# Cross-attention block: the last 82 context rows multiplied in two contraction tiles instead of three products

## The chip, the cores and the metric

The kernel runs on one core of one Trainium2 chip. The metric is the device time of that core in microseconds (us). The kernel before takes 300.28 us (median of 3 runs, 299.73 to 300.45); one further run was recorded by the hardware profiler, and all rows in this document come from that one.

## What is computed

For each of B = 8 batches there are N = 100 query rows of width D = 1024 and M = 722 context rows of width C = 512. Cut to what matters:

```python
memory_proj = einsum('bme,de->bmd', memory, W_mem)
scores = einsum('bnd,bmd->bnm', hidden_states, memory_proj) / sqrt(D)
attn = softmax(scores, axis=-1)
memory_context = einsum('bnm,bmd->bnd', attn, memory_proj)
gate = sigmoid(einsum('bnf,df->bnd', concat([hidden_states, memory_context]), W_gate) + b_gate)
out = rmsnorm(hidden_states + gate * memory_context, norm_w)
```

The kernel never forms `memory_proj`. It multiplies the queries with `W_mem` first (giving `q`, width 512), takes scores against the raw context, multiplies the probabilities with the raw context (giving 100 x 512 per batch, called `pc`), and multiplies that with `W_mem` afterwards (giving `mc`). The step that is changed is probabilities times raw context: for each batch a product over 722 context rows.

## The kernel before

**Three products for one.** Every large float32 product is made from operands split in two: `hi` is the operand copied by ScalarE (ACT) into the narrower format float32r, `lo` is what remains (operand minus `hi`, by VectorE, DVE), also float32r. A product is `hi*hi + hi*lo + lo*hi`, three matmuls on TensorE (PE) that accumulate in one PSUM bank.

**Stages.** First the query projection (to 42.4 us), then `for b in range(B): step(b, ...)`, one batch each, then the projection to `mc`, the gate and the normalisation. In a step PE runs, in this order: scores (L384, 24 matmuls), some matmuls of the gate's x half to fill time (`fill(1)`, L290), the six transposes of the probabilities (L398), `fill(2)` (L290), the probabilities times the context (L408), `fill(3)` (L290), four transposes of `pc` (L415). The fills run over 3, 3 and 1 of 8 blocks; in step 0 they run over 3, 2 and 1, with 2 ahead of the scores.

**The product over 722 rows.** 722 rows are `MT = 5` tiles of 128 and a last one of `ML = 82`. Each tile costs three matmuls, 18 in all; each streams 512 columns, whether the tile has 128 rows or 82. PE waits for `pt_lo_done` ahead of tile 0 and for `cn_lo_done` ahead of tiles 0 and 3.

**Who makes the operands.** The context rows are loaded into `cn_stage` by DMAs that SyncE (SP) issues: tiles 0 to 2 (L217), tiles 3 and 4 (L221), the 82 rows (L223). ACT makes `cn_hi` (L542 for tiles 0 to 2; L545 and L546 for the rest) and DVE `cn_lo` (all its subtractions have the helper's line, L711). The probabilities come transposed out of PSUM: ACT writes `pt_hi` (L600 for five tiles, L602 for the 82 rows, `pt_hi_done`), then DVE `pt_lo` (`pt_lo_done`). In step b ACT's order is: exponential, a weight split (L523), L545, L546, L600, L602, the two `ct_hi` (L534, the transposed context for the next step's scores), then `pc` (L607). DVE's order is: maxima, weight split, `pt_lo`, `cn_lo` of tiles 3 to 5, the two `ct_lo`.

**SP's order.** SP issues one DMA after another, and waits in place. For batch b + 1: a gate weight, two halves of `ct_stage` (L210), L217, then (after `cn_lo_done` of batch b's second part, since the buffer is single) L221 and L223. After the last batch's context come the weights `w_mem_t` 1 to 3.

Of the kernel before, what the change touches and what calls it, by code (L numbers as in the profile page):

```python
# [5 lines left out]
B, N, D = 8, 100, 1024  # L6
M, C = 722, 512
# [3 lines left out]
KD, KC = D // P, C // P  # L11
MT = M // P
ML = M - MT * P
MH = M // 2
BANK = 512
WB = KD * P
# [26 lines left out]
def build(nc, xT, ctxT, ctxN, w_mem, w_gate_x, w_mem_t, w_gate_mc, b_gate, norm_w, outT, out_rows):  # L43
# [4 lines left out]
    with top:  # L48
# [18 lines left out]
        bias_t = sb(top, "bias_t", [P, KD])  # L67
        norm_t = sb(top, "norm_t", [P, KD])
        table_probe = sb(top, "table_probe", [P, 1])
        idle_work = sb(top, "idle_work", [P, P], mybir.dt.bfloat16)  # L70
        top_score = sb(top, "top_score", [N, 2])
        neg_top = sb(top, "neg_top", [N, 1])
# [3 lines left out]

        with ExitStack() as attn:
            ct_stage = sb(attn, "ct_stage", [P, KC, M])
            cn_stage = sb(attn, "cn_stage", [P, MT + 1, C])
            ct_hi = sb(attn, "ct_hi", [P, KC, M], F32R)  # L80
            ct_lo = sb(attn, "ct_lo", [P, KC, M], F32R)
            cn_hi = sb(attn, "cn_hi", [P, MT + 1, C], F32R)
            cn_lo = sb(attn, "cn_lo", [P, MT + 1, C], F32R)
            probs = sb(attn, "probs", [N, M])
            pt_hi = sb(attn, "pt_hi", [P, MT + 1, N], F32R)
            pt_lo = sb(attn, "pt_lo", [P, MT + 1, N], F32R)
            pc = sb(attn, "pc", [N, C])
# [56 lines left out]
        first_hi_done, first_lo_done = sem("first_hi_done"), sem("first_lo_done")  # L144
        ct_hi_done, ct_lo_done = sem("ct_hi_done"), sem("ct_lo_done")
        cn_hi_done, cn_lo_done = sem("cn_hi_done"), sem("cn_lo_done")
        q_hi_done, q_lo_done = sem("q_hi_done"), sem("q_lo_done")
        pt_hi_done, pt_lo_done = sem("pt_hi_done"), sem("pt_lo_done")
        at_hi_done, at_lo_done = sem("at_hi_done"), sem("at_lo_done")
# [45 lines left out]
        @block.sync  # L195
        def _(sp):
            def load_x(k):
                sp.dma_start(acc[:, k, :], xT[k * P:(k + 1) * P, :]).then_inc(x_in[k], 16)

            def load_w(j, src, slot):  # L200

                if not isinstance(j, int) or j >= 2:
                    sp.wait_ge(w_lo_done, j - 1)
                sp.dma_start(w_stage[:, slot, :], src).then_inc(w_in[slot], 16)

            def load_ctxT(b, first=False):
                for s in range(2):
                    if not first:
                        sp.wait_ge(ct_lo_done, 2 * b - 1 + s)
                    sp.dma_start(ct_stage[:, 2 * s:2 * s + 2, :],  # L210
                                 ct_rows[bass.ds(b * C + s * 2 * P, 2 * P), :]
                                 .rearrange("(k p) m -> p k m", p=P)).then_inc(ct_in[s], 16)

            def load_ctx(b, first=False):
                if not first:
                    sp.wait_ge(cn_lo_done, 2 * b - 1)
                sp.dma_start(cn_stage[:, 0:3, :], cn_rows[bass.ds(b * M, 3 * P), :]  # L217
                             .rearrange("(t p) c -> p t c", p=P)).then_inc(cn_in[0], 16)
                if not first:
                    sp.wait_ge(cn_lo_done, 2 * b)  # L220
                sp.dma_start(cn_stage[:, 3:MT, :], cn_rows[bass.ds(b * M + 3 * P, (MT - 3) * P), :]  # L221
                             .rearrange("(t p) c -> p t c", p=P)).then_inc(cn_in[1], 16)
                sp.dma_start(cn_stage[0:ML, MT, :],  # L223
                             cn_rows[bass.ds(b * M + MT * P, ML), :]).then_inc(cn_in[1], 16)


            sp.dma_start(acc[:, 0, 0:H], xT[0:P, 0:H]).then_inc(x_first_in, 16)
            for i in range(2):
                cols = slice(i * C // 2, (i + 1) * C // 2)
                sp.dma_start(w_stage[:, 0, cols], w_mem[0][:, cols]).then_inc(w_first_in[i], 16)  # L230
            sp.dma_start(acc[:, 0, H:R], xT[0:P, H:R]).then_inc(x_in[0], 16)
            sp.dma_start(w_stage[:, 0, C:WB], w_mem[0][:, C:WB]).then_inc(w_in[0], 16)
            sp.dma_start(acc[:, 1, 0:H], xT[P:2 * P, 0:H]).then_inc(x_second_in, 16)
            sp.dma_start(acc[:, 1, H:R], xT[P:2 * P, H:R]).then_inc(x_in[1], 16)
            load_x(2)
            load_w(1, w_mem[1], 1)
            load_x(3)
            load_x(4)
            load_x(5)
            load_w(2, w_mem[2], 0)  # L240
            load_x(6)
            load_x(7)
            load_w(3, w_mem[3], 1)
            load_ctxT(0, first=True)
            load_ctx(0, first=True)
            sp.dma_start(bias_t[:, :], b_gate).then_inc(const_in, 16)
            sp.dma_start(norm_t[:, :], norm_w).then_inc(const_in, 16)
            load_w(J_GX, w_gate_x[0], 0)
            load_w(J_GX + 1, w_gate_x[1], 1)


            def ahead(b, slot):
                load_w(J_GX + 2 + b, wgx_rows[bass.ds((b + 2) * P, P), :], slot)
                load_ctxT(b + 1)
# [12 lines left out]

            sp.wait_ge(mc_made, 1)
            sp.dma_start(x_again[:, :, :], xT.rearrange("(k p) r -> p k r", p=P)).then_inc(xa_in, 16)
            for t in range(1, KD):  # L270
                load_w(J_G2 + t, w_gate_mc[t], t % 2)
            for k in range(0, KD, 2):
                sp.wait_ge(out_done, k + 2)
                sp.dma_start(out_v[:, k:k + 2, :], acc[:, k:k + 2, 0:FIRST]).then_inc(stored, 16)
            for i in range(ROWS2):
                sp.wait_ge(row_left, i + 1)
                sp.wait_ge(row_right, i + 1)
                sp.dma_start(out_rows[i * CHUNK:(i + 1) * CHUNK, :],
                             row_out[:, i * D:(i + 1) * D]).then_inc(stored, 16)
            sp.wait_ge(stored, 16 * (KD // 2 + ROWS2))  # L280
# [3 lines left out]
        def _(pe):  # L284
# [80 lines left out]
            def step(b, slot, cuts):  # L365
# [34 lines left out]
                fill(2)  # L400

                pe.wait_ge(pt_lo_done, b + 1)
                for t in range(MT + 1):
                    if t in (0, 3):
                        pe.wait_ge(cn_lo_done, 2 * b + 1 + t // 3)
                    rows = P if t < MT else ML
                    for lhs, rhs, part in ((pt_hi, cn_hi, 0), (pt_hi, cn_lo, 1), (pt_lo, cn_hi, 2)):
                        done = nc.tensor.matmul(bank(PCB, C, N), lhs[0:rows, t, :], rhs[0:rows, t, :],  # L408
                                                start=t == 0 and part == 0, stop=t == MT and part == 2)
                done.then_inc(pc_made, 1)  # L410
                fill(3)

# [102 lines left out]
        def _(act):  # L515
# [21 lines left out]
            def split_ctx(b, part):  # L537
                if part == 0:
                    if not isinstance(b, int) or b > 0:
                        act.wait_ge(pc_made, b)  # L540
                    act.wait_ge(cn_in[0], 16 * b + 16)
                    nc.scalar.activation(cn_hi[:, 0:3, :], cn_stage[:, 0:3, :], ACT.Copy).then_inc(cn_hi_done, 1)  # L542
                else:
                    act.wait_ge(cn_in[1], 32 * b + 32)
                    nc.scalar.activation(cn_hi[:, 3:MT, :], cn_stage[:, 3:MT, :], ACT.Copy)  # L545
                    nc.scalar.activation(cn_hi[0:ML, MT, :], cn_stage[0:ML, MT, :],  # L546
                                         ACT.Copy).then_inc(cn_hi_done, 1)

            act.wait_ge(x_first_in, 16)
            nc.scalar.activation(act_hi[:, 0, 0:H], acc[:, 0, 0:H], ACT.Copy).then_inc(first_hi_done, 1)  # L550
# [158 lines left out]
        def _(dve):  # L709
# [18 lines left out]
            def split_ctx(b, part):  # L728
                dve.wait_ge(cn_hi_done, 2 * b + part + 1)
                if part == 0:  # L730
                    minus(cn_lo[:, 0:3, :], cn_stage[:, 0:3, :], cn_hi[:, 0:3, :]).then_inc(cn_lo_done, 1)
                else:
                    minus(cn_lo[:, 3:MT, :], cn_stage[:, 3:MT, :], cn_hi[:, 3:MT, :])
                    minus(cn_lo[0:ML, MT, :], cn_stage[0:ML, MT, :], cn_hi[0:ML, MT, :]).then_inc(cn_lo_done, 1)

            nc.vector.memset(idle_work[:, :], 0.0).then_inc(idle_work_set, 1)
            dve.wait_ge(first_hi_done, 1)
# [19 lines left out]
            split_x(6)  # L757
            split_x(7)
            split_w(3, 1)
            split_ctxT(0)  # L760
            split_ctx(0, 0)
            split_ctx(0, 1)
# [157 lines left out]
        def _(pool):  # L920
            nc.gpsimd.memset(ident[:, :], 0.0).then_inc(ident_zeroed, 1)
            pool.wait_ge(ident_zeroed, 1)
            nc.gpsimd.affine_select(out=ident[:, :], in_=ident[:, :], compare_op=ALU.not_equal, fill=1.0,
                                    base=0, pattern=[[-1, P]], channel_multiplier=1).then_inc(consts_set, 1)


            pool.wait_ge(mean_w_set, 4)
# [36 lines left out]
```

## Time and profile before

| what | value |
|---|---|
| median of 3 runs | 300.28 us (299.73 to 300.45) |
| the profiled run, its time | 300.07 us |
| its span (first to last instruction) | 298.3 us |
| PE busy | 292.5 us (98%), 1674 matmuls |
| ACT busy | 156.4 us (52%) |
| DVE busy | 164.1 us (55%) |
| TensorE clock granted, mean | 0.996 of full |
| chain that ended last | PE 98%, of which L290 69%, L408 11%, L384 11% |

The profile's chain of waits goes back from the last instruction to whatever released each one. Matmuls overlap in the pipeline, so one is recorded as about 0.39 us long while the next starts 0.23 us after it. The cost of one matmul in a stream is the distance between starts, or the length of a piece of the chain by its count, never the recorded duration. "PEld" is the loading of a matmul's stationary operand, which runs beside the matmul before it. "SPq" rows are DMA issues on SP.

### The profile page before, as it was taken

The page shows a single profiled execution, that of the slowest core. Times are in us where ns is not written, and L with a number is a line of the kernel's source. Part 1 is how long each engine was busy: PE and PEld are TensorE (multiplying, and loading weights), DVE is VectorE, ACT ScalarE, POOL GpSimd, SP SyncE. Part 2 cuts the span into 40 slices and gives each one's busy share as a digit, 9 for nine tenths or more (in the row PEclk, how much of TensorE's full clock was granted, in tenths as well). Part 3 has the DMA queues.
Part 4 walks back from the last instruction along what each step waited for, and adds up shares of the span by engine and source line. Part 5 has one row for each costly group of instructions (what it writes and reads, how often), then busy time and mean ns, then how long its engine had stood idle before and what let it go on. Part 6 is the DMA issues. An engine that isn't in the chain of part 4 may idle for free.

```text
span 298.3 us, 4078 instructions
## 1 busy us (share of the span) xinstructions
PE 292.5 (98%) x1674; PEld 281.3 (94%) x1674; DVE 164.1 (55%) x232; ACT 156.4 (52%) x227; POOL 3.0 (1%) x9
## 2 busy tenths in 40 slices
PE   8999999999999999999999999999999999999993
PEld 8999999898999989899898989999999999999993
DVE  3657454557575565855557553423457662543663
ACT  5547345454573736548363525543467773643563
POOL 0000000000000000000000000000000000010001
PEclk9999999999999999999999999999999999999998
DMA  6998391644729467383944020177223400000235
GB/s 207 406 369 268 105 357 34 229 132 135 243 99 313 149 210 247 98 265 116 288 182 145 20 70 8 64 286 294 74 70 142 141 2 1 0 2 8 109 114 211
DMA packets 18450, 46.34 MB, mean 155 GB/s; under 512 B 1520, under 2 KB 3312, under 8 KB 18432
## 3 DMA queue, kind: packets, MB, share of 16 engines
q1 hardware_dynamic: 18432, 46.09, 45.2%
q8 instruction: 13, 0.21, 0.3%
q14 instruction: 5, 0.04, 0.0%
HBM read 42.80 MB, written 3.28 MB: 154 GB/s over the span
## 4 chain that ended last, share of the span: by engine, by line
PE 98%; DVE 0%; issue 0%; DVEq 0%
PE ps L290 69%; PE ps L408 11%; PE ps L384 11%; PE ps L398 1%; PE ps L304 1%; PE ps L415 1%; PE ps L488 1%; PE ps L315 0%; PE ps L318 0%; PE ps L476 0%; DVE x_again L911 0%; PE ps L325 0%; PE ps L330 0%; PE ps L321 0%; PE ps L327 0%; PE ps L468 0%
## 5 line engine op out<-in xcount | busy, mean ns | idle before, releaser
L290 PE MATMUL ps<-act_hi,w_hi 128*128 128x400 f32 (+4 forms) x272 | 79.5, 342 | 0.0
L290 PE MATMUL ps<-act_hi,w_lo 128*128 128x400 f32 (+4 forms) x272 | 78.9, 340 | 0.0
L290 PE MATMUL ps<-act_lo,w_hi 128*128 128x400 f32 (+4 forms) x272 | 78.8, 340 | 0.0
L290 PEld LDWEIGHTS ps<-act_hi,w_hi 128*128 128x128 f32 x272 | 49.9, 188 | 0.9
L290 PEld LDWEIGHTS ps<-act_lo,w_hi 128*128 128x128 f32 x272 | 50.6, 188 | 0.1
L290 PEld LDWEIGHTS ps<-act_hi,w_lo 128*128 128x128 f32 x272 | 50.6, 188 | 0.0
L711 DVE TENSOR_TENSOR w_lo<-w_stage,w_hi 128x1024 fp32r<-128x1024 f32 (+2 forms) x23 | 26.0, 1131 | 24.3 <-ACT w_hi L523 23.2
L711 DVE TENSOR_TENSOR cn_lo<-cn_stage,cn_hi 128x1536 fp32r<-128x1536 f32 (+2 forms) x24 | 28.6, 1217 | 6.4 <-ACT cn_hi L542 5.6
L711 DVE TENSOR_TENSOR ct_lo<-ct_stage,ct_hi 128x1444 fp32r<-128x1444 f32 x16 | 25.8, 1654 | 0.5 <-ACT ct_hi L534 0.5
L523 ACT ACTIVATE w_hi<-w_stage 128x1024 fp32r<-128x1024 f32 x20 | 21.0, 1054 | 6.7 <-PE ps L290 4.9
L607 ACT ACTIVATE pc<-ps,row_inv 100x512 f32<-100x512 f32 x8 | 5.5, 687 | 34.3 <-PE ps L408 34.3
L534 ACT ACTIVATE ct_hi<-ct_stage 128x1444 fp32r<-128x1444 f32 x16 | 21.7, 1408 | 0.0
L664 ACT ACTIVATE gate<-ps,bias_t 128x384 f32<-128x384 f32 (+3 forms) x15 | 8.6, 570 | 24.6 <-PE ps L290 24.5
L384 PE MATMUL ps<-ct_hi,q_hi 128*100 128x362 f32 x64 | 21.4, 334 | 0.0
L593 ACT ACTIVATE probs<-ps,neg_top 100x722 f32<-100x722 f32 x8 | 6.9, 865 | 27.2 <-DVE neg_top L782 27.2
L384 PE MATMUL ps<-ct_hi,q_lo 128*100 128x362 f32 x64 | 21.0, 328 | 0.0
L849 DVE TENSOR_TENSOR gate<-gate,mc 128x416 f32<-128x416 f32 (+3 forms) x17 | 9.3, 550 | 21.1 <-ACT gate L664 21.1
L384 PE MATMUL ps<-ct_lo,q_hi 128*100 128x362 f32 x64 | 20.9, 327 | 0.0
L711 DVE TENSOR_TENSOR act_lo<-mc,act_hi 128x800 fp32r<-128x800 f32 x8 | 7.9, 993 | 20.5 <-ACT mc L635 20.5
L408 PE MATMUL ps<-cn_hi,pt_hi 128*100 128x512 f32 (+1 forms) x48 | 18.9, 394 | 0.0
L408 PE MATMUL ps<-cn_hi,pt_lo 128*100 128x512 f32 (+1 forms) x48 | 18.8, 392 | 0.0
L408 PE MATMUL ps<-cn_lo,pt_hi 128*100 128x512 f32 (+1 forms) x48 | 18.8, 391 | 0.0
(105 smaller groups left out, 446.2 us busy)
## 6 DMA issues: line engine op xcount, KB each, us to landing
ct_stage<-ctxT SPq DMA_DIRECT2D x16, 722.0 KB, 9.8
cn_stage<-ctxN SPq DMA_DIRECT2D x8, 768.0 KB, 5.8
cn_stage<-ctxN SPq DMA_DIRECT2D x8, 512.0 KB
w_stage<-w_gate_x SPq DMA_DIRECT2D x8, 512.0 KB, 8.9
w_stage<-w_gate_mc SPq DMA_DIRECT2D x8, 512.0 KB, 3.6
x_again<-xT SPq DMA_DIRECT2D x1, 3200.0 KB, 11.3
acc<-xT SPq DMA_DIRECT2D x6, 400.0 KB, 7.9
w_stage<-w_mem_t SPq DMA_DIRECT2D x4, 512.0 KB, 5.6
```

Source lines behind the costliest of these rows:

```text
L290: done = nc.tensor.matmul(o, wgt, stream[h][part], start=first and wgt is wh and part == 0, stop=last and wgt is wl, skip_group_check=onto)
L304: nc.tensor.matmul(bank(7, P), idle_work[:, :], idle_work[:, :], start=True, stop=True)
L384: done = nc.tensor.matmul(bank(h, MH + 1, N), lhs[:, k, b * N:(b + 1) * N], rhs[:, k, at:at + MH + 1], start=k == 0 and part == 0, stop=k ...
L398: done = nc.tensor.transpose(o, probs[:, t * P:t * P + rows], ident[0:N, 0:N])
L408: done = nc.tensor.matmul(bank(PCB, C, N), lhs[0:rows, t, :], rhs[0:rows, t, :], start=t == 0 and part == 0, stop=t == MT and part == 2)
L523: nc.scalar.activation(w_hi[home][:, :], w_stage[:, slot, :], ACT.Copy).then_inc(w_hi_done, 1)
L534: nc.scalar.activation(ct_hi[:, 2 * s:2 * s + 2, :], ct_stage[:, 2 * s:2 * s + 2, :], ACT.Copy).then_inc(ct_hi_done, 1)
L593: nc.scalar.activation(probs[:, :].rearrange("p (h m) -> p h m", h=2), scores, ACT.Exp, bias=neg_top[:, :], scale=float(D) ** -0.5, accum_ ...
L607: nc.scalar.activation(pc[:, :], bank(PCB, C, N), ACT.Copy, scale=row_inv[:, :]).then_inc(pc_scaled, 1)
L664: nc.scalar.activation(part, part if n < 2 else gate_bank(n), ACT.Sigmoid, bias=bias_t[:, t:t + 1]).then_inc(gate_done, 1)
L711: return nc.vector.tensor_tensor(out, whole, hi.bitcast(F32), ALU.subtract)
L849: nc.vector.tensor_tensor(part, part, mc[:, t, r0:r1], ALU.mult).then_inc(gated, 1)
```

## The change

The three products of the last 82 rows have 3 x 82 = 246 rows to contract, and these fit into two tiles of up to 128 rows. With `SPILL = 42` and `REST = 40`:

- tile `MT`: rows 0 to 81 are `pt_hi` against `cn_hi`; rows 82 to 123 are `pt_hi` of rows 0 to 41 against `cn_lo` of rows 0 to 41
- tile `MT + 1`: rows 0 to 81 are `pt_lo` against `cn_hi`; rows 82 to 121 are `pt_hi` of rows 42 to 81 against `cn_lo` of rows 42 to 81

The context side is loaded from memory in this layout (82 rows twice, by a broadcast source, and once more as 42 and 40 rows at partition 82): four DMAs in place of one. ACT writes `sign * stage` over 124 rows x 1024 columns, with sign -1 in rows below 82 and +1 above; DVE then writes `stage * low_rows - that` in place, which is `hi` below row 82 and `lo` above. The probabilities' side is made as before, and two small DMAs inside SBUF copy `pt_hi` rows to partition 82 onward of `pt_hi` and `pt_lo` (`move_pt`); PE waits for both (`pt_moved`) ahead of the last two matmuls. `low_rows` and `hi_sign` are computed once on DVE, and GpSimd zeroes the spare rows once.

```diff
@@ sync
+            def move_pt(b):
+                sp.wait_ge(pt_hi_done, b + 1)
+                sp.dma_start(pt_hi[ML:ML + SPILL, MT, :].bitcast(F32),
+                             pt_hi[0:SPILL, MT, :].bitcast(F32)).then_inc(pt_moved, 16)
+                sp.dma_start(pt_lo[ML:ML + REST, MT, :].bitcast(F32),
+                             pt_hi[SPILL:ML, MT, :].bitcast(F32)).then_inc(pt_moved, 16)
...
                 if not first:
+                    move_pt(b - 1)
                     sp.wait_ge(cn_lo_done, 2 * b)
                 sp.dma_start(cn_stage[:, 3:MT, :], cn_rows[bass.ds(b * M + 3 * P, (MT - 3) * P), :]
                              .rearrange("(t p) c -> p t c", p=P)).then_inc(cn_in[1], 16)
-                sp.dma_start(cn_stage[0:ML, MT, :],
-                             cn_rows[bass.ds(b * M + MT * P, ML), :]).then_inc(cn_in[1], 16)
+                at = b * M + MT * P
+                if first:
+                    sp.wait_ge(spare_zeroed, 1)
+                for a, n in ((0, ML - 2), (ML - 2, 2)):
+                    sp.dma_start(cn_stage[a:a + n, MT:MT + 2, :], cn_rows[at + a:at + a + n, :].unsqueeze(1)
+                                 .to_broadcast([n, 2, C])).then_inc(cn_end_in, 16)
+                sp.dma_start(cn_stage[ML:ML + SPILL, MT, :], cn_rows[at:at + SPILL, :]).then_inc(cn_end_in, 16)
+                sp.dma_start(cn_stage[ML:ML + REST, MT + 1, :],
+                             cn_rows[at + SPILL:at + ML, :]).then_inc(cn_end_in, 16)
...
             load_w(J_MC + 1, w_mem_t[1], 1)
+            move_pt(B - 1)
             load_w(J_MC + 2, w_mem_t[2], 0)
@@ tensor
-                for t in range(MT + 1):
+                for t in range(MT):
                     if t in (0, 3):
                         pe.wait_ge(cn_lo_done, 2 * b + 1 + t // 3)
...
+                pe.wait_ge(pt_moved, 32 * (b + 1))
+                for i, (lhs, rows) in enumerate(((pt_hi, ML + SPILL), (pt_lo, ML + REST))):
+                    done = nc.tensor.matmul(bank(PCB, C, N), lhs[0:rows, MT, :], cn_hi[0:rows, MT + i, :],
+                                            start=False, stop=i == 1)
@@ scalar
-                    act.wait_ge(cn_in[1], 32 * b + 32)
+                    act.wait_ge(cn_in[1], 16 * b + 16)
                     nc.scalar.activation(cn_hi[:, 3:MT, :], cn_stage[:, 3:MT, :], ACT.Copy)
-                    nc.scalar.activation(cn_hi[0:ML, MT, :], cn_stage[0:ML, MT, :],
-                                         ACT.Copy).then_inc(cn_hi_done, 1)
+                    act.wait_ge(cn_end_in, 64 * b + 64)
+                    act.wait_ge(hi_sign_set, 1)
+                    rows = slice(0, ML + SPILL)
+                    nc.scalar.activation(cn_hi[rows, MT:MT + 2, :], cn_stage[rows, MT:MT + 2, :], ACT.Copy,
+                                         scale=hi_sign[rows, :]).then_inc(cn_hi_done, 1)
@@ vector
-                    minus(cn_lo[0:ML, MT, :], cn_stage[0:ML, MT, :], cn_hi[0:ML, MT, :]).then_inc(cn_lo_done, 1)
+                    packed = cn_hi[0:ML + SPILL, MT:MT + 2, :]
+                    nc.vector.scalar_tensor_tensor(packed, cn_stage[0:ML + SPILL, MT:MT + 2, :],
+                                                   low_rows[0:ML + SPILL, :], packed.bitcast(F32), ALU.mult,
+                                                   ALU.subtract).then_inc(cn_lo_done, 1)
...
+            dve.wait_ge(consts_set, 1)
+            nc.vector.reduce_sum(low_rows[:, :], ident[:, ML:P], AX.X).then_inc(low_rows_set, 1)
+            dve.wait_ge(low_rows_set, 1)
+            nc.vector.tensor_scalar(hi_sign[:, :], low_rows[:, :], 2.0, -1.0, ALU.mult, ALU.add)\
+                .then_inc(hi_sign_set, 1)
@@ gpsimd
+            pool.wait_ge(consts_set, 1)
+            nc.gpsimd.memset(cn_stage[96:P, MT:MT + 2, :], 0.0).then_inc(spare_zeroed, 1)
```

On PE, the end of the product over the context in step 0, before (the last three are the 82-row tile, L290 is `fill(3)`, L415 the transposes of `pc`):

```order
L408 MATMUL ps<-cn_hi,pt_lo 100x512
L408 MATMUL ps<-cn_hi,pt_hi 100x512
L408 MATMUL ps<-cn_lo,pt_hi 100x512
L408 MATMUL ps<-cn_hi,pt_lo 100x512
L290 MATMUL ps<-act_hi,w_hi 128x400 x2
L290 MATMUL ps<-act_lo,w_hi 128x400 x2
L290 MATMUL ps<-act_hi,w_lo 128x400 x2
L415 MATMUL ps<-ident,pc 128x100 [waits pc_scaled]
```

The same place after (L431 is the old L408, L435 the packed tiles, L314 the old L290, L442 the old L415):

```order
L431 MATMUL ps<-cn_hi,pt_lo 100x512
L435 MATMUL ps<-cn_hi,pt_hi 100x512 [waits pt_moved]
L435 MATMUL ps<-cn_hi,pt_lo 100x512
L314 MATMUL ps<-act_hi,w_hi 128x400 x2
L314 MATMUL ps<-act_lo,w_hi 128x400 x2
L314 MATMUL ps<-act_hi,w_lo 128x400 x2
L442 MATMUL ps<-ident,pc 128x100 [waits pc_scaled]
```

One matmul of three is gone, and the first of the two that remain waits for the moved rows.

On SP, the issues of one steady step, before:

```order
L204 DMA w_stage<-w_gate_x 128x1024 [waits w_lo_done]
L210 DMA ct_stage<-ctxT 128x2x722 [waits ct_lo_done] x2
L217 DMA cn_stage<-ctxN 128x3x512 [waits cn_lo_done]
L221 DMA cn_stage<-ctxN 128x2x512 [waits cn_lo_done]
L223 DMA cn_stage<-ctxN 82x512
```

and after:

```order
L211 DMA w_stage<-w_gate_x 128x1024 [waits w_lo_done]
L217 DMA ct_stage<-ctxT 128x2x722 [waits ct_lo_done] x2
L232 DMA cn_stage<-ctxN 128x3x512 [waits cn_lo_done]
L224 DMA pt_hi<-pt_hi 42x100 [waits pt_hi_done]
L226 DMA pt_lo<-pt_hi 40x100
L237 DMA cn_stage<-ctxN 128x2x512 [waits cn_lo_done]
L243 DMA cn_stage<-ctxN 80x2x512
L243 DMA cn_stage<-ctxN 2x2x512
L245 DMA cn_stage<-ctxN 42x512
L246 DMA cn_stage<-ctxN 40x512
```

Two small copies stand between the two context loads, and four loads stand where one stood.

## Rows read from the trace of the kernel before

**Rows 1.** The page, part 1 (busy us, share, instructions) and part 2.
```profile
PE 292.5 (98%) x1674; PEld 281.3 (94%) x1674; DVE 164.1 (55%) x232; ACT 156.4 (52%) x227; POOL 3.0 (1%) x9
...
PEclk9999999999999999999999999999999999999998
```

**Rows 2.** The chain that ended last: start us, us, what (step 3, then step 4).
```profile
105.55 4.13 PE ps L408 x18
109.68 1.09 PE ps L290 x6
...
123.25 4.18 PE ps L408 x18
```

**Rows 3.** The instructions of L408, one of three alike: duration ns, forms.
```profile
L408 PE MATMUL ps<-cn_hi,pt_hi x48: 389/394/398, 52.3 to 179.7; 128*100 128x512 f32 x40, 82*100 82x512 f32 x8
```

**Rows 4.** Timeline of step 3, loads of PE's stationary operand: start us, us.
```profile
105.21 0.16 PEld L408 LDWEIGHTS ps<-cn_hi,pt_hi 128*100 128x100 f32 x1
...
107.23 0.16 PEld L408 LDWEIGHTS ps<-cn_hi,pt_hi 128*100 128x100 f32 x1
...
108.60 0.16 PEld L408 LDWEIGHTS ps<-cn_hi,pt_hi 82*100 82x100 f32 x1
...
110.87 0.17 PEld L384 LDWEIGHTS ps<-ct_hi,q_hi 128*100 128x100 f32 x1
```

**Rows 5.** Timeline of step 3, ACT and DVE: start us, us, idle before.
```profile
101.44 0.62 ACT L546 ACTIVATE cn_hi<-cn_stage 82x512 fp32r<-82x512 f32 x1
102.30 0.59 ACT L600 ACTIVATE pt_hi<-ps 128x500 fp32r<-128x500 f32 x1 [0.23 <-PE ps L398]
102.78 0.24 ACT L602 ACTIVATE pt_hi<-ps 82x100 fp32r<-82x100 f32 x1
...
103.06 0.84 DVE L711 TENSOR_TENSOR pt_lo<-ps,pt_hi 128x500 fp32r<-128x500 f32 x2 [1.13 <-ACT pt_hi L602]
103.82 1.81 DVE L711 TENSOR_TENSOR cn_lo<-cn_stage,cn_hi 128x1024 fp32r<-128x1024 f32 x2
105.56 3.22 DVE L711 TENSOR_TENSOR ct_lo<-ct_stage,ct_hi 128x1444 fp32r<-128x1444 f32 x2
```

**Rows 6.** Groups by shape: busy us, mean ns, idle before.
```profile
L711 DVE TENSOR_TENSOR cn_lo<-cn_stage,cn_hi 128x1024 fp32r<-128x1024 f32 x8 | 9.7, 1213 | 0.8 <-ACT cn_hi L546 0.8
...
L711 DVE TENSOR_TENSOR cn_lo<-cn_stage,cn_hi 82x512 fp32r<-82x512 f32 x8 | 5.4, 680 | 0.0
...
L545 ACT ACTIVATE cn_hi<-cn_stage 128x1024 fp32r<-128x1024 f32 x8 | 8.4, 1053 | 1.4 <-DMA cn_stage<-ctxN 1.4
...
L546 ACT ACTIVATE cn_hi<-cn_stage 82x512 fp32r<-82x512 f32 x8 | 4.9, 616 | 0.0
```

**Rows 7.** Timeline of step 3, the issues on SP around `cn_lo`.
```profile
97.55 0.37 SPq L217 DMA_DIRECT2D cn_stage<-ctxN  x1
105.66 0.37 SPq L221 DMA_DIRECT2D cn_stage<-ctxN  x1
```

**Rows 8.** Timeline of step 0: the end of `pt_hi`, the first 82-row load.
```profile
50.80 0.24 ACT L602 ACTIVATE pt_hi<-ps 82x100 fp32r<-82x100 f32 x1
...
55.53 0.16 PEld L408 LDWEIGHTS ps<-cn_hi,pt_hi 82*100 82x100 f32 x1
```

**Rows 9.** DMA issues: count, KB each, median us from issue to landing.
```profile
ct_stage<-ctxT SPq DMA_DIRECT2D x16, 722.0 KB, 9.8
cn_stage<-ctxN SPq DMA_DIRECT2D x8, 768.0 KB, 5.8
...
outT<-acc SPq DMA_DIRECT2D x4, 416.0 KB, 2.5
```

**Rows 10.** Windows: busy by engine (PE, PEld, DVE, ACT, POOL), clock, DMA share, GB/s.
```profile
104.00:105.00 1.00, 1.00 (x7) 1.00 (x6) 1.00 (x2) 1.00 (x2) 0.00 (x0) 1.00 0.00 0
115.00:116.00 1.00, 1.00 (x7) 1.00 (x6) 1.00 (x3) 0.00 (x0) 0.00 (x0) 1.00 0.14 53
```

**Rows 11.** Timeline of DVE ahead of step 0: idle time before the first `q_lo`.
```profile
37.07 1.13 DVE L711 TENSOR_TENSOR q_lo<-ps,q_hi 128x400 fp32r<-128x400 f32 x2 [3.06 <-ACT q_hi L584]
```

More of the change, by code:

```diff
@@ L13 @@
 ML = M - MT * P
+SPILL, REST = 42, ML - 42
 MH = M // 2
@@ L69, in build @@
         table_probe = sb(top, "table_probe", [P, 1])
+        low_rows = sb(top, "low_rows", [P, 1])
+        hi_sign = sb(top, "hi_sign", [P, 1])
         idle_work = sb(top, "idle_work", [P, P], mybir.dt.bfloat16)
@@ L78, in build @@
             ct_stage = sb(attn, "ct_stage", [P, KC, M])
-            cn_stage = sb(attn, "cn_stage", [P, MT + 1, C])
+            cn_stage = sb(attn, "cn_stage", [P, MT + 2, C])
             ct_hi = sb(attn, "ct_hi", [P, KC, M], F32R)
             ct_lo = sb(attn, "ct_lo", [P, KC, M], F32R)
-            cn_hi = sb(attn, "cn_hi", [P, MT + 1, C], F32R)
-            cn_lo = sb(attn, "cn_lo", [P, MT + 1, C], F32R)
+            cn_hi = sb(attn, "cn_hi", [P, MT + 2, C], F32R)
+            cn_lo = sb(attn, "cn_lo", [P, MT, C], F32R)
             probs = sb(attn, "probs", [N, M])
@@ L146, in build @@
         cn_hi_done, cn_lo_done = sem("cn_hi_done"), sem("cn_lo_done")
+        spare_zeroed, low_rows_set, hi_sign_set = sem("spare_zeroed"), sem("low_rows_set"), sem("hi_sign_set")
+        cn_end_in, pt_moved = sem("cn_end_in"), sem("pt_moved")
         q_hi_done, q_lo_done = sem("q_hi_done"), sem("q_lo_done")
@@ L402, in step @@
                 pe.wait_ge(pt_lo_done, b + 1)
-                for t in range(MT + 1):
+                for t in range(MT):
                     if t in (0, 3):
                         pe.wait_ge(cn_lo_done, 2 * b + 1 + t // 3)
-                    rows = P if t < MT else ML
                     for lhs, rhs, part in ((pt_hi, cn_hi, 0), (pt_hi, cn_lo, 1), (pt_lo, cn_hi, 2)):
-                        done = nc.tensor.matmul(bank(PCB, C, N), lhs[0:rows, t, :], rhs[0:rows, t, :],
-                                                start=t == 0 and part == 0, stop=t == MT and part == 2)
+                        nc.tensor.matmul(bank(PCB, C, N), lhs[:, t, :], rhs[:, t, :],
+                                         start=t == 0 and part == 0, stop=False)
+                pe.wait_ge(pt_moved, 32 * (b + 1))
+                for i, (lhs, rows) in enumerate(((pt_hi, ML + SPILL), (pt_lo, ML + REST))):
+                    done = nc.tensor.matmul(bank(PCB, C, N), lhs[0:rows, MT, :], cn_hi[0:rows, MT + i, :],
+                                            start=False, stop=i == 1)
                 done.then_inc(pc_made, 1)
```

## The prediction

> **What bounds the kernel now.** I read the page first, then the chain of waits, then one steady step (step 3, 93.4 to 111.1 us) in the timeline. The page shows PE busy 98% of the span while ACT and DVE are busy about half, and the clock row shows full speed in nearly every slice [rows 1]. So TensorE runs at its upper level of 2.4 GHz with nothing to win or lose there. The chain of waits is PE work from end to end, and its pieces follow each other without a gap: in step 3 the product over the context starts at 105.55 and takes 4.13 us, and `fill(3)` starts at 109.68, which is 105.55 + 4.13 [rows 2]. PE is the bound in each of the 8 steps. A matmul taken out of this stream is therefore worth its full spacing, as long as nothing that PE waits for comes later than PE wants it. The rest of the argument is how much room each such operand has.
>
> **What is removed.** L408 has 3 x 48 matmuls, 8 of each 48 with 82 rows, and these take as long as those with 128 (one range of 389 to 398 ns for both forms) [rows 3]. The spacing is 4.13 us / 18 = 0.2294 us (0.2322 in step 4) [rows 2]. One of 18 goes in each of 8 steps: 8 x 0.23 = 1.84 us. The two packed tiles have 124 and 122 rows instead of 82; since 128-row tiles keep the same spacing, I take no extra cost for that.
>
> **What PE's new wait costs.** `pt_moved` must arrive when PE loads the first packed tile. In the run before, that place is 108.60 [rows 4], and it stays there, since the removed matmul comes behind it. The chain to it is: ACT ends `pt_hi` at 102.78 + 0.24 = 103.02 [rows 5]; SP wakes and issues the first copy about 0.03 later (that is the distance from the end of `cn_lo`, 103.82 + 1.81 = 105.63, to the issue at 105.66), and the second 0.41 later [rows 5, 7]. With 0.1 us for ACT's own delay (below) the second issue is at 103.56. This leaves 5.04 us for it to land. SP is free: its last issue was at 97.55 [rows 7]. The DMA engines are idle then, 0.00 busy from 104 to 105 [rows 10]. In step 0, `fill(2)` is shorter: from 50.80 + 0.24 + 0.44 = 51.48 to 55.53 leaves 4.05 us [rows 8]. No copy inside SBUF is in the trace. The nearest rows by size are far larger: 416 KB land in 2.5 us, 768 KB in 5.8 [rows 9]. The copies hold 16 KB each, so I take 2.5 or less, with 5.8 as the other end. At 2.5 the wait costs nothing, with 1.5 us to spare in step 0 and 2.5 elsewhere.
>
> **What ACT and DVE do more.** ACT's L546 of 82 x 512 (616 ns) becomes one of 124 x 1024, which I price as L545 (1053 ns): 0.44 us more per step [rows 6]. ACT was idle 0.23 us before `pt_hi` and its instructions overlap a little: L546 would now run from 101.44 to 102.49, `pt_hi` starts near 102.4 instead of 102.30, so about 0.1 us later [rows 5]. DVE's 82 x 512 (680 ns) becomes a scalar_tensor_tensor of 124 x 1024. No such instruction is in the trace; the nearest row is the subtraction of 128 x 1024 on the same tiles, 1213 ns [rows 6]: 0.53 us more. Then:
> `pt_lo` ends at 103.06 + 0.84 + 0.1 = 104.0; PE wants it at 105.21, 1.2 us of room [rows 4, 5].
> `cn_lo` ends at 105.63 + 0.53 + 0.1 = 106.26; PE wants it ahead of tile 3 at 107.23, 1.0 us of room [rows 4, 5].
> `ct_lo` ends at 105.56 + 3.22 + 0.63 = 109.41; PE wants it for the next scores, at 110.87 before and 110.64 with a matmul less, 1.2 us of room [rows 4, 5].
> All three are hidden; if this cover were gone, the added 0.63 us per step would outweigh the 0.23 won.
>
> Here a rule speaks against the change. The Trainium skill, "Vector Engine (DVE) Microarchitecture Reference", section "Points that are easy to get wrong", says that this instruction with two SBUF sources that are not bf16 runs at half throughput. The existing subtraction also has two float32 sources in SBUF, and the trace gives no row of the other. What such an outcome would do is rival A.
>
> **What the loads do more.** Each batch now loads 492 KB in place of 164 (2 x 82 + 82 rows of 2 KB), 328 KB more. On SP, L221 goes out 0.63 later, at 106.3, followed by four issues at 0.41 us instead of one: the last at 107.9, the first half of `ct_stage` near 108.7 instead of 107.2. The packed rows are read by ACT 17.70 us (the period of the steps, 123.25 - 105.55) after 101.44, at 119.1 [rows 2, 5]: 11.2 us after the last issue, against landings of 9.8 for the slowest loads now [rows 9]. `ct_stage` before landed at 107.2 + 9.8 = 117.0; with 1.5 for the later issue and 328 KB at about 300 GB/s, 1.1 us, it lands at 119.6, and ACT begins on it after `pt_hi` of step 4, at 103.02 + 17.70 + 0.1 = 120.8. So I price the loads at nothing, with about 1.2 us of cover in front of ACT, and the 1.2 us of `ct_lo` behind it.
>
> The tail of the loads is visible: from 115 to 116 us the DMA engines are 0.14 busy at 53 GB/s, as if 2 of 16 (0.125) still worked [rows 10]. The Trainium skill, "DMA: Bandwidth & Descriptors", section "Why a DMA increments its semaphore by 16 and not by 1", says that a transfer is spread over the largest number of engines up to 16 that divides its outer size: that is 2 for 82 rows, and 16, 14 and 10 for the new pieces of 80, 42 and 40. The row agrees with 2 engines; by the rule the tail goes away and the loads land sooner rather than later, which makes rival C less likely.
>
> **Start and end.** Ahead of step 0 there are two small DVE instructions, the larger ACT and DVE operations for batch 0, four loads more and 328 KB more. DVE is idle 3.06 us before the first `q_lo` [rows 11]. My sum of what could add up there is 0.5 + 0.44 + 0.53 + 1.1 for data, 2.6 us, so it is covered, though with little left. The load of batch 1's tiles 3 and 4 now stands behind step 0's copies, at about 52 us instead of 36; ACT reads it in step 1, where L546 falls on 101.44 - 2 x 17.70 = 66.0 [rows 2, 5]. The last copy stands ahead of two `w_mem_t` loads, which are used only after the next stage begins. Both cost nothing.
>
> **The sum.** 1.84 us off, nothing added. Against the profiled run: 300.07 - 1.84 = 298.23. That run was 0.21 below the median, and from the median it is 300.28 - 1.84 = 298.44. I forecast 298.4, a gain of 0.6%. About 0.3% (0.9 us) is what a measurement of this kernel can tell from no change.
>
> **Rivals.**
> A. *The scalar_tensor_tensor is half as fast.* From [rows 6] a column costs (1213 - 680) / 512 = 1.04 ns and an instruction 0.15 us beside, so 1024 columns at half rate take 2.28 us. `cn_lo` then ends at 105.63 - 0.68 + 2.28 + 0.1 = 107.33, past the 107.23 that PE wants, and with the semaphore's way a stall of 0.1 to 0.2 us in 7 steps (step 0's was long done): 298.44 + 1.05 = 299.5. `ct_lo` would end at 110.5, just in time. The same data path and types as the existing subtraction speak against it. Chance 0.08.
> B. *The moved rows land late* (the slower side). PE stands still by L - 5.04 us in 7 steps and L - 4.05 in step 0, where L is the landing of the second copy. The whole gain is gone at 8 L = 39.3 + 1.84, L = 5.15 us. At 6.0, a little above what 768 KB take [rows 9], it costs 8.7 us and the kernel takes 307.1. For it speaks that PE now waits on a DMA issued in the same step, which no step did before; against it, the idle engines [rows 10] and the size. Chance 0.05.
> C. *`ct_stage` or the packed rows land late.* This needs landings about 2.4 us worse than I took. If they were 1 us beyond that in 6 steps: 304.4. Chance 0.05.
> D. *Part of the gain goes at the start or in small waits.* A start later than its 3.06 us of cover by half a microsecond, or 0.06 us at each new wait: 298.9 to 299.1. Chance 0.07.
>
> **How the numbers follow.** The forecast has 0.75, and with it 298.0 to 298.9 (the runs lie from 0.55 below to 0.17 above their median, and spacing between 0.229 and 0.232). The range goes from 297.9, and takes in D and the nearer half of A: up to 299.5. B, C and the far half of A lie outside. Faster by over 0.3% (under 299.4): 0.75 + 0.07 less a little = 0.79. Within 0.3%: A, and small cases of B and C, 0.12. Slower: 0.09.
>
> **What would show it.** PE's piece of the chain in each step should read about 3.90 us for 17 matmuls, with the step's period down from 17.70 to 17.47. No gap should stand ahead of the packed tiles; a gap there is B, a gap ahead of the tenth matmul is A, one ahead of the scores is C. The scalar_tensor_tensor should read 1.2 us, the ACT copy 1.05 us, the moves 2.5 us or less to landing. I am wrong if PE is busy less than 98% between 42 and 182 us.

## The result and the profile after

The changed kernel takes 298.98 us (median of 8 runs, 297.93 to 299.24) against 300.13 us (8 runs, 299.73 to 300.45): the ratio is 0.9967, 95% interval 0.9957 to 0.9978. The medians are 1.15 us apart, the ratio stands for 1.0 us (0.7 to 1.3), and 1.84 was forecast. The time lies in the range of 297.9 to 299.5, and just outside the 298.0 to 298.9 that the forecast alone had.

The profiled execution of the changed kernel has a span of 296.0 us, 2.3 less than before, and at 297.93 us it is the fastest of the eight. Its rows must be read with that in mind, so a second profile of the same kernel stands among the experiments. First the chain of waits after, from the first large piece (start us, us, what); the context product is L431 and L435, the old L290 is L314, the old L384 is L408:

```profile
8.85 32.77 PE ps L314 x180
41.62 3.98 PE ps L408 x24
...
104.14 3.47 PE ps L431 x15
107.61 0.47 PE ps L435 x2
108.08 1.09 PE ps L314 x6
...
121.64 3.48 PE ps L431 x15
...
179.56 82.20 PE ps L314 x447
```

The chain is still PE from end to end, and no gap stands ahead of L435: 104.14 + 3.47 = 107.61. PE is busy all the time between 42 and 182 us. The step's period went from 17.70 us [rows 2] to 121.64 - 104.14 = 17.50, 0.20 less and not 0.23. The reason is in the first line of the pair: 15 matmuls take 3.47 to 3.48 us, 0.232 each, where [rows 2] gave 0.229. In six of the eight steps they take 3.47 to 3.49 us, in steps 2 and 7 they take 3.43.

The timeline of step 3 after, in the order of [rows 4], [rows 5] and [rows 7] (start us, us, idle before):

```profile
100.04 1.14 ACT L576 ACTIVATE cn_hi<-cn_stage,hi_sign 124x1024 fp32r<-124x1024 f32 x1
101.81 0.79 SPq L224 DMA_DIRECT2D pt_hi<-pt_hi  x1
102.64 0.72 SPq L226 DMA_DIRECT2D pt_lo<-pt_hi  x1
103.71 1.27 DVE L765 SCALAR_TENSOR_TENSOR cn_hi<-cn_stage,low_rows,cn_hi 124x1024 fp32r<-124x1024 f32 x1
104.91 3.22 DVE L741 TENSOR_TENSOR ct_lo<-ct_stage,ct_hi 128x1444 fp32r<-128x1444 f32 x2
105.82 0.16 PEld L431 LDWEIGHTS ps<-cn_hi,pt_hi 128*100 128x100 f32 x1
...
107.22 0.17 PEld L435 LDWEIGHTS ps<-cn_hi,pt_hi 124*100 124x100 f32 x1
...
109.27 0.17 PEld L408 LDWEIGHTS ps<-ct_hi,q_hi 128*100 128x100 f32 x1
```

The scalar_tensor_tensor takes 1.27 us (1.2 forecast), the ACT copy 1.14 (1.05 forecast). `cn_lo` ends at 104.98 and PE wants it at 105.82, so 0.84 us of room are left (1.0 forecast). `ct_lo` ends at 108.13 and PE starts to load for the next scores at 109.27, 1.1 us of room (1.2 forecast). A copy inside SBUF keeps SP busy for 0.79 and 0.72 us, twice the 0.37 of a large load [rows 7]. DMA issues after, as in [rows 9]:

```profile
ct_stage<-ctxT SPq DMA_DIRECT2D x16, 722.0 KB, 8.4
cn_stage<-ctxN SPq DMA_DIRECT2D x8, 768.0 KB, 5.8
```

`ct_stage` lands in 8.4 us instead of 9.8, although 328 KB more are loaded per batch.

So nothing waits that did not wait before, PE has 8 matmuls fewer, and yet 0.7 to 0.8 us of 1.84 are missing. Two theories: the rest of the change costs something that no wait shows (loads, copies, larger instructions), or the gain of a removed matmul was over-priced.

### The profile page after: what moved, and what is told of

Read it like the earlier page. It is cut to its first block, busy times and chain, and to the rows that moved or that the text cites. A ratio compares the mean times of both kernels' runs of the same rounds, so it can differ in the third digit from the quotient of the medians.

```text
span 296.0 us, 4113 instructions
## 1 busy us (share of the span) xinstructions
PE 290.2 (98%) x1666; PEld 279.4 (94%) x1666; DVE 169.1 (57%) x234; ACT 159.9 (54%) x227; POOL 4.0 (1%) x10
## 4 chain that ended last, share of the span: by engine, by line
PE 98%; DVE 0%; issue 0%; DVEq 0%
PE ps L314 70%; PE ps L408 11%; PE ps L431 9%; PE ps L422 1%; PE ps L435 1%; PE ps L328 1%; PE ps L442 1%; PE ps L515 1%; PE ps L503 0%; PE ps L339 0%; DVE x_again L949 0%; PE ps L345 0%; PE ps L349 0%; PE ps L342 0%; PE ps L354 0%; PE ps L351 0%
## 5 line engine op out<-in xcount | busy, mean ns | idle before, releaser
L314 PE MATMUL ps<-act_hi,w_hi 128*128 128x400 f32 (+4 forms) x272 | 79.8, 343 | 0.0
L314 PE MATMUL ps<-act_hi,w_lo 128*128 128x400 f32 (+4 forms) x272 | 79.0, 340 | 0.0
L314 PE MATMUL ps<-act_lo,w_hi 128*128 128x400 f32 (+4 forms) x272 | 78.9, 340 | 0.0
L314 PEld LDWEIGHTS ps<-act_hi,w_hi 128*128 128x128 f32 x272 | 49.9, 188 | 1.0
L314 PEld LDWEIGHTS ps<-act_lo,w_hi 128*128 128x128 f32 x272 | 50.6, 188 | 0.1
L314 PEld LDWEIGHTS ps<-act_hi,w_lo 128*128 128x128 f32 x272 | 50.6, 188 | 0.1
L741 DVE TENSOR_TENSOR cn_lo<-cn_stage,cn_hi 128x1536 fp32r<-128x1536 f32 (+1 forms) x16 | 23.8, 1486 | 7.2 <-ACT cn_hi L569 5.6
L408 PE MATMUL ps<-ct_hi,q_hi 128*100 128x362 f32 x64 | 21.4, 335 | 0.0
L408 PE MATMUL ps<-ct_hi,q_lo 128*100 128x362 f32 x64 | 21.0, 328 | 0.0
L408 PE MATMUL ps<-ct_lo,q_hi 128*100 128x362 f32 x64 | 21.0, 328 | 0.0
L314 PE MATMUL ps<-q_hi,w_hi 128*128 128x400 f32 x64 | 17.5, 344 | 0.0
L314 PE MATMUL ps<-q_lo,w_hi 128*128 128x400 f32 x64 | 17.5, 344 | 0.0
L314 PE MATMUL ps<-q_hi,w_lo 128*128 128x400 f32 x64 | 17.4, 344 | 0.0
```

The source lines that it names most:

```text
L314: done = nc.tensor.matmul(o, wgt, stream[h][part], start=first and wgt is wh and part == 0, stop=last and wgt is wl, skip_group_check=onto)
L408: done = nc.tensor.matmul(bank(h, MH + 1, N), lhs[:, k, b * N:(b + 1) * N], rhs[:, k, at:at + MH + 1], start=k == 0 and part == 0, stop=k ...
L741: return nc.vector.tensor_tensor(out, whole, hi.bitcast(F32), ALU.subtract)
```

## Experiments

All ratios are to the kernel before on the same chip, with their 95% intervals.

**1. The changed kernel again, and the kernel before again.** No edit.

> The changed kernel, unaltered. Forecast 1.84 us off; the 8 runs gave 1.15 us (300.13 to 298.98), the two profiled executions 2.14 (300.07 to 297.93). Theory 1 (start luck): the profiled execution of the changed kernel began its first full matmul of the projection 0.95 us earlier (8.85 against 9.80 us into the span) than that of before, which is chance; a second profile starts near 9.8 and its span is near 297.0. Theory 2 (the change itself starts PE earlier): a second profile starts at 8.85 again. Either way the 8 steps take 137.9 us against 139.5, as in the first profile, and the ratio lies in 0.9957 to 0.9978.

> The kernel before, unaltered, as a control against itself: ratio 1.000 within 0.001. Its profile shows how far the start (9.80 us to the first matmul of L290) and the 8 steps (42.51 to 182.04, 139.53 us) move from one execution to the next. Theory 1 expects a start that moves by up to 1 us, theory 2 a start at 9.8 within 0.1. Both expect 139.5 for the steps.

Measured: 0.9964 (0.9951 to 0.9976) for the changed kernel, 0.9999 (0.9991 to 1.0008) for the control. Chain of waits, the changed kernel's second profile, then the control's:

```profile
9.57 32.71 PE ps L314 x180
...
180.22 82.18 PE ps L314 x447
```

```profile
9.65 32.84 PE ps L290 x180
...
181.96 81.98 PE ps L290 x447
```

In the changed kernel the projection's long piece started at 8.85 us once and at 9.57 the second time, so the early start was chance. Over all profiles of this study where that piece of 180 is in the chain, with and without the change, it started between 8.85 and 10.3 us. The parts behind the start repeat well. The 8 steps (from the first scores to the last long piece) take 137.94 us in both profiles of the changed kernel, against 139.53 and 139.47: 1.6 us less. The last long piece has the same 447 matmuls in the same order and takes 82.18 to 82.20 against 81.98 to 81.99: 0.2 us more. The change does not touch that stage.

**2. The matmul alone, and all but the matmul.** One product of the last 82 rows left out of the kernel before (`pt_lo` times `cn_hi`):

```diff
                     for lhs, rhs, part in ((pt_hi, cn_hi, 0), (pt_hi, cn_lo, 1), (pt_lo, cn_hi, 2)):
+                        if t == MT and part == 2:
+                            continue
```

> The kernel before with one of the three products of the last 82 rows left out (pt_lo times cn_hi), and nothing else: the removal of the matmul alone, with none of the loads, copies, waits or larger ACT and DVE instructions. Theory S (the stream sets the price): 8 x 0.229 = 1.84 us off in the steps if nothing was added by the rest, ratio 0.9939. Theory E (a matmul less is itself worth less than its spacing, since the others then stand wider): the same 1.15 us as the full change, ratio 0.9962. If S holds, the rest of the change costs about 0.7 us.

and the changed kernel with the second packed matmul issued twice:

```diff
-                for i, (lhs, rows) in enumerate(((pt_hi, ML + SPILL), (pt_lo, ML + REST))):
-                    done = nc.tensor.matmul(bank(PCB, C, N), lhs[0:rows, MT, :], cn_hi[0:rows, MT + i, :],
-                                            start=False, stop=i == 1)
+                for i, (lhs, rows) in enumerate(((pt_hi, ML + SPILL), (pt_lo, ML + REST), (pt_lo, ML + REST))):
+                    done = nc.tensor.matmul(bank(PCB, C, N), lhs[0:rows, MT, :], cn_hi[0:rows, MT + min(i, 1), :],
+                                            start=False, stop=i == 2)
```

> The changed kernel with the second packed matmul issued twice, so that PE has as many matmuls as before while all the rest of the change is in. Its output is not the reference's. The rest alone then stands against the kernel before. Theory S: about 0.7 us slower than before, ratio 1.002. Theory E: the same as before, ratio 1.000 within 0.001. A stall at the moved rows or at cn_lo would show as a gap in the chain at those places; neither theory expects one.

Measured: 0.9944 (0.9931 to 0.9957), 1.7 us off; and 1.0024 (1.0014 to 1.0034), 0.7 us on. Chain of the first, then of the second:

```profile
42.18 3.99 PE ps L384 x24
...
52.15 3.91 PE ps L410 x17
...
179.97 81.99 PE ps L290 x447
```

```profile
42.97 3.98 PE ps L408 x24
...
182.81 82.19 PE ps L314 x447
```

The two add to the changed kernel's result. A removed matmul is worth its spacing or nearly so, and the rest of the change costs 0.7 us. In the first kernel the steps take 137.79 us; in the second they take 139.84, and no gap stands anywhere in them.

**3. Where things lie in SBUF.** `low_rows` and `hi_sign` are allocated between `table_probe` and `idle_work`, and each takes a slot of 32 bytes per partition (that is how the program lays out tiles). Everything allocated later lies 64 bytes further, in the last stage too. The kernel before with nothing but that:

```diff
         table_probe = sb(top, "table_probe", [P, 1])
+        spare_a = sb(top, "spare_a", [P, 1])
+        spare_b = sb(top, "spare_b", [P, 1])
```

> The kernel before with two unused one-column tiles allocated where the change puts low_rows and hi_sign, so that everything allocated behind them lies 64 bytes further, as in the changed kernel; no instruction differs. The earlier profiles show two losses that no wait explains: the last stage's chain piece of 447 matmuls takes 82.18 to 82.20 us in all three kernels with the change against 81.98 to 81.99 in the three without, and the first 15 matmuls of the context product 3.48 against 3.44. Theory L (placement in SBUF): this kernel shows the last stage at 82.2 and the context product at 4.18 instead of 4.13 per step, 0.2 to 0.6 us slower, ratio 1.001 to 1.002. Theory W (the added work: loads, copies, larger ACT and DVE instructions): both numbers as before, ratio 1.000.

Measured: 1.0016 (1.0008 to 1.0025), 0.5 us slower with no instruction changed. The start and the end of the steps in its chain:

```profile
42.60 3.98 PE ps L386 x24
...
182.44 82.19 PE ps L292 x447
```

Its context products take 4.17 to 4.19 us in all eight steps, where [rows 2] has 4.13 and 4.18; the kernel before has 4.13 in six of eight in one profile and in seven of eight in the other, and which steps read 4.18 differs from kernel to kernel. The steps take 139.84 us here, and 139.84 in the kernel of experiment 2 that has the whole change and no matmul less; the last piece takes 82.19 us in both. So these 64 bytes account, within 0.01 us of the chain, for all that the rest of the change costs behind the start. The counter-test is the changed kernel with these two tiles allocated behind the attention's last one:

```diff
-        low_rows = sb(top, "low_rows", [P, 1])
-        hi_sign = sb(top, "hi_sign", [P, 1])
...
             pc = sb(attn, "pc", [N, C])
+            low_rows = sb(attn, "low_rows", [P, 1])
+            hi_sign = sb(attn, "hi_sign", [P, 1])
```

> The changed kernel with low_rows and hi_sign allocated behind the attention's last tile, so that the tiles of the last stage lie at the same addresses as before; no instruction differs. Theory L: the last stage's piece returns from 82.19 to 81.98, the context product perhaps too, ratio to before 0.9945 to 0.9957. Theory W: as the changed kernel, 0.9964, last stage 82.19.

Measured: 298.04 us, 0.9936 (0.9924 to 0.9948), 1.9 us off: the whole forecast gain. Its chain:

```profile
42.44 3.99 PE ps L408 x24
...
52.42 3.44 PE ps L431 x15
...
179.99 81.99 PE ps L314 x447
```

The 15 matmuls read 3.44 us in every step, the last piece at 81.99, and the 8 steps take 137.55 us. This version is faster than both kernels of the case.

**4. Loads alone, and the change without its copies.** The kernel before with the four loads of the change (the diff's lines on `cn_stage` and `cn_end_in`) and all else as it was:

> The kernel before with the context's last rows loaded as the change does (four DMAs, 492 KB in place of 164, the larger cn_stage) and everything else as it was: three matmuls, 82-row ACT and DVE instructions, no copies. Theory W, loads: the context product at 4.18 per step or a later start of the steps, 0.3 to 0.7 us slower. Theory L: the last stage's addresses are those of before, so 81.98 there, and ratio 1.000 within 0.001. On landings: if the 82-row load was slow since it used 2 of 16 DMA engines, the 0.14 busy microsecond at its end goes and ct_stage lands sooner than 9.8 us.

Measured: 1.0001 (0.9992 to 1.0009), steps 139.54 us, last piece 81.98. The loads cost nothing. They land sooner: 7.9 us for `ct_stage`. The window at the same time as the second row of [rows 10] (the steps began 0.55 us earlier here):

```profile
115.00:116.00 1.00, 1.00 (x7) 1.00 (x7) 0.83 (x3) 0.10 (x1) 0.00 (x0) 1.00 1.02 393
```

The microsecond in which 0.14 of the DMA engines worked at 53 GB/s is now one with all busy at 393 GB/s, already on the next load. The changed kernel without `move_pt` (these rows of `pt_hi` and `pt_lo` zeroed once on DVE):

```diff
                 if not first:
-                    move_pt(b - 1)
...
-                pe.wait_ge(pt_moved, 32 * (b + 1))
+                pe.wait_ge(pt_moved, 2)
```

> The changed kernel without the two copies of the probabilities' rows (these rows of pt_hi and pt_lo are set to zero once, so the products hi*lo of the last 82 rows are left out). Theory W, copies: 0.3 to 0.7 us faster than the changed kernel, ratio 0.994 to 0.9955. Theory L, and my forecast that the copies are hidden: the same as the changed kernel, 0.9964 within 0.001, the context product still 3.48 + 0.47.

Measured: 0.9962 (0.9950 to 0.9973), the same as the changed kernel; the context product reads 3.48 + 0.47 as there. The copies and PE's wait for them cost nothing.

**5. Which operand's place counts.**

```diff
+            spare_p = sb(attn, "spare_p", [P, 16])
             probs = sb(attn, "probs", [N, M])
...
+        spare_w = sb(top, "spare_w", [P, 16])
         w_hi.append(sb(top, "w_hi2", [P, WB], F32R))
```

> The kernel before with two unused spaces of 64 bytes: one ahead of probs, which moves pt_hi and pt_lo (the stationary operands of the context product), one ahead of w_hi2, which moves w_hi2, w_lo2, w_hi3 and w_lo3 (stationary operands in the last stage); cn_hi, cn_lo and all others stay. No instruction differs. Theory St (the stationary operand's place counts): the context product goes from 4.13 to 4.17 to 4.19 us per step and the last stage from 81.98 to 82.19, as with all tiles moved. Theory Mv (the moving operand's place counts): both stay.

```diff
+            spare_c = sb(attn, "spare_c", [P, 16])
             ct_stage = sb(attn, "ct_stage", [P, KC, M])
...
+            spare_p = sb(attn, "spare_p", [P, 48])
             probs = sb(attn, "probs", [N, M])
```

> The kernel before with 64 unused bytes ahead of ct_stage and 192 ahead of probs: cn_hi, cn_lo, ct_hi and ct_lo (moving operands) lie 64 bytes further, pt_hi and pt_lo 256 bytes, the last stage's tiles not at all. No instruction differs. Theory Mv: the context product at 4.17 to 4.19 us per step. Theory St: 4.13. Both: last stage 81.98.

Measured: 1.0036 (1.0020 to 1.0052) and 1.0012 (0.9996 to 1.0029). Chain of the first, then of the second:

```profile
52.74 4.20 PE ps L410 x18
...
182.78 82.19 PE ps L292 x447
```

```profile
52.98 4.14 PE ps L410 x18
...
70.68 4.19 PE ps L410 x18
...
182.70 81.98 PE ps L292 x447
```

With the stationary operands 64 bytes further (and `probs` and `pc` with them, which the product does not read), all eight context products take 4.18 to 4.20 us and the last piece 82.19: the full effect, in both stages. For the last stage that settles it, since only `w_hi2`, `w_lo2`, `w_hi3` and `w_lo3` were moved there, and the trace shows the loss inside the piece of 447. Before, then in the first kernel, the first matmul whose weights are `w_hi2`, and the first after it whose weights lie in the unmoved `q_hi`:

```profile
216.71 0.35 PE L290 MATMUL ps<-act_hi,w_hi 128*128 128x416 f32 x1
...
234.44 0.35 PE L290 MATMUL ps<-act_hi,q_hi 128*128 128x416 f32 x1
```

```profile
217.44 0.35 PE L292 MATMUL ps<-act_hi,w_hi 128*128 128x416 f32 x1
...
235.30 0.35 PE L292 MATMUL ps<-act_hi,q_hi 128*128 128x416 f32 x1
```

The 192 matmuls ahead of this stretch take 34.67 and 34.66 us, the stretch takes 17.73 and 17.86. By the starts of single matmuls, 0.12 us arise in the first 72 of this stretch, whose weights lie in the moved tiles, 0.08 in the 48 that read these tiles later in the piece, and no more than 0.01 in all others. So the matmuls that read a moved weight tile are the slower ones, and not the stage as a whole. In the second kernel three products take 4.14 and five 4.18 to 4.19, between the two theories. Whether that is the moving operands' 64 bytes or the 256 bytes by which `pt_hi` moved there, these runs do not tell.

**6. The room of the two waits.** The copies made, waited for and made again:

```diff
+                sp.wait_ge(pt_moved, 64 * b + 32)
+                sp.dma_start(pt_hi[ML:ML + SPILL, MT, :].bitcast(F32),
+                             pt_hi[0:SPILL, MT, :].bitcast(F32)).then_inc(pt_moved, 16)
+                sp.dma_start(pt_lo[ML:ML + REST, MT, :].bitcast(F32),
+                             pt_hi[SPILL:ML, MT, :].bitcast(F32)).then_inc(pt_moved, 16)
```

> The changed kernel with the two copies of the probabilities' rows made, waited for on SP, and made once more before PE may go on: the time from pt_hi to PE's permission is doubled. With l the landing of a copy from its own issue, PE stands still by 2 l - 3.75 us in steps 1 to 7 (5.41 us of room from the first issue at 101.81 to the load at 107.22, less two issue distances of 0.83) and by 2 l - 2.76 in step 0. My forecast took l as at most 2.5. At l = 2.0: 0.25 x 7 + 1.24 = 3.0 us slower than the changed kernel; at 1.5: 0.2 us slower; at 2.5: 11 us slower. The wait that SP shows between the two pairs gives l itself. The rival that the copies are far from hurting would show no gap at all.

Measured: 0.9992 (0.9978 to 1.0006), 0.9 us more than the changed kernel; the steps take 138.86 us against 137.94. The chain now leaves PE in step 0:

```profile
50.38 0.88 SPq L224
...
51.30 1.91 DMA pt_lo<-pt_hi
...
53.23 0.75 SPq L230
...
54.01 1.90 DMA pt_lo<-pt_hi
...
55.96 0.71 PE ps L441 x2
```

This gives the landing that no row of before had: 1.91 us from the start of the issue of the second copy. Twice of that costs step 0 about 0.9 us and the other steps almost nothing; by my formula, with l = 1.91, it should have been 1.06 there and 0.07 in each other step.

One DVE subtraction more:

```diff
-                    minus(cn_lo[:, 3:MT, :], cn_stage[:, 3:MT, :], cn_hi[:, 3:MT, :])
+                    minus(cn_lo[:, 3:MT, :], cn_stage[:, 3:MT, :], cn_hi[:, 3:MT, :]).then_inc(once_done, 1)
+                    dve.wait_ge(once_done, b + 1)
+                    minus(cn_lo[:, 3:MT, :], cn_stage[:, 3:MT, :], cn_hi[:, 3:MT, :])
```

> The changed kernel with one more DVE subtraction of 128 x 1024 (the one of tiles 3 and 4 done twice) ahead of the scalar_tensor_tensor, about 1.17 us more: this tests the room I gave cn_lo. In the profile after, it ends at 104.98 and PE loads the tenth matmul of the context product at 105.82, 0.84 us of room. So a gap of 0.3 to 0.4 us must stand ahead of the tenth matmul in 7 steps, 2.3 to 2.8 us slower than the changed kernel. If ct_lo decides instead, the gap stands ahead of the scores: it ends at 108.13 + 1.17 = 109.3 against 109.27, so under 0.1 there. If there is no gap, PE's waits have more room than the profile shows.

Measured: 1.0036 (1.0019 to 1.0053), steps 140.33 us, 2.4 more than the changed kernel. What PE's loads wait for, over the whole run (us in total, times, longest), and the place in step 2:

```profile
PEld ps L432 <- DVE cn_hi L768: 3.8, 7, 0.6
```

```profile
89.24 0.16 PEld L432 LDWEIGHTS ps<-cn_hi,pt_lo 128*100 128x100 f32 x1
89.94 0.16 PEld L432 LDWEIGHTS ps<-cn_hi,pt_hi 128*100 128x100 f32 x1 [0.54 <-DVE cn_hi L768]
```

The gap stands where forecast, ahead of the tenth matmul, in 7 steps. 0.70 us lie between two loads that are 0.23 apart otherwise, of which PE's stream loses some 0.34 us a step (2.4 over 7). This is the cover that the change draws on: it was 1.6 us before (105.63 against 107.23) and is 0.84 after.

## Why the prediction was right or wrong, point by point

- **A matmul is worth its spacing.** Right: 1.7 us for 8 of them, measured alone, and 1.9 with the change at its old addresses (1.84 forecast).
- **No extra cost for packed tiles.** Right within the trace: the two take 0.47 us, where two others take 0.46.
- **The copies are hidden.** Right, and now measured: leaving them out changes nothing. They land in 1.9 us, against at most 2.5 taken. SP's issue takes 0.72 to 0.88 us, not 0.41, which used 0.3 to 0.5 us of the room and made no difference. At the first step the second copy is issued at 51.09 and PE loads the first packed tile at 54.68, so it lands about 1.7 us early (51.09 + 1.91 = 53.0). Rival B is out.
- **ACT, DVE.** Right in kind, a little small in size: 1.14 and 1.27 us for 1.05 and 1.21. Rival A is out: at half the rate of the subtraction the scalar_tensor_tensor would have taken 2.28 us by my estimate. The rule of the Trainium skill, "Vector Engine (DVE) Microarchitecture Reference", section "Points that are easy to get wrong", does not show here if it is read as half of that rate, as I read it. The room for `cn_lo` was real and narrow, as the added subtraction in experiment 6 shows.
- **The loads.** Right that they cost nothing, wrong in direction: I let `ct_stage` take 1.1 us longer to land, and it takes 1.4 less. What I took as rival C's brake turned out to be the main effect. The rule of "DMA: Bandwidth & Descriptors" in the Trainium skill, section "Why a DMA increments its semaphore by 16 and not by 1", says that a DMA gets the largest number of engines up to 16 that divides its slowest dimension, which makes 2 for 82 rows and 16, 2, 14 and 10 for the pieces of 80, 2, 42 and 40. The trace agrees on the 82 rows, with 0.14 busy before; that the tail is gone shows as 1.02 in that window with the new loads, while no row here shows the number of engines of each new piece.
- **The start.** No cost was found there. DVE's idle time before the first `q_lo` went from 3.06 us [rows 11] to 1.43, and PE's start moves by over 1 us from run to run for reasons outside the change.
- **"1.84 us off, nothing added."** This is the step that failed, though the time fell into the range. It took every cost to be an instruction, a wait or a transfer. What was added is a place: two one-column tiles moved all later tiles by 64 bytes, and PE's stream became wider by up to 0.003 us a matmul. By the chains this is 137.94 - 137.55 = 0.39 us in the steps and 0.2 in the last stage, 0.6 us; by the timed ratios of the changed kernel's repetition (0.9964) and of the one with the two tiles allocated last (0.9936), 0.8 us. Rival D put 0.07 on "part of the gain goes at the start or in small waits", with the right time (298.9 to 299.1) and the wrong mechanism. That 298.98 lies in the range is in part luck: the range reached beyond 298.9 for stalls at the start, at new waits and on DVE, and none of these was found.

The chains account for 1.4 us of gain in the changed kernel (1.59 in the steps less 0.2 in the last piece), the timed runs for 1.0 to 1.1. The 0.3 us between them is within the second interval (0.7 to 1.5 us) and just outside the first (0.7 to 1.3); it stays open.

## What to carry to other kernels

When one engine is busy from end to end, price a removed instruction at its spacing, and check for each operand of what remains how much earlier it is ready than wanted. Here this gave 1.84 us, and 1.7 and 1.9 were measured in the two kernels where nothing had moved. Where a change adds even a tiny tile, compare the addresses of all others before and after: put new small tiles behind the old ones, and if a stage that the edit does not touch gets slower, pad the old kernel by the same bytes as a test. One profile of each kernel was not enough to see the loss, as the start alone moved by 0.7 us between two profiles of the same kernel; comparing single stages of the chain was.

## What the hardware showed that I had not expected

- Moving tiles in SBUF by 64 bytes changed the speed of matmuls that no other engine held up. With the stationary operands moved, the 18 matmuls of the context product take 4.18 to 4.20 us instead of mostly 4.13, and the 447 matmuls of the projection and gate 82.19 instead of 81.98, all but 0.01 of it in the 120 whose weights lie in the moved tiles. Which property of the address matters is not settled. By the sizes and the order of the allocations, addresses went from 96 to 32 modulo 128 (`w_hi2`, `w_hi3`) and from 32 to 96 (`pt_hi`), so no single one of these remainders is the good one. In the context product even the kernel before reads 4.18 instead of 4.13 in one or two steps of eight, so there the address changes how often the slower value comes, for a reason that no run here shows.
- Issuing an SBUF to SBUF copy of 42 or 40 rows of 400 bytes holds SP for 0.79 and 0.72 us, a load of 512 KB for 0.37.
- A load of 82 rows that is issued as 80 + 2 (and two further pieces) lets the loads queued behind it land sooner: 7.9 instead of 9.8 us for `ct_stage`, with more bytes in all.
